# A fused two-layer cross-attention and expert kernel: experts' weights in 48 separately placed parts, and 128 instead of 96 early wide products

## The reference

```
xt = layernorm(x)
router_scores = softmax(xt @ Wr + br)
fs = _grouped_routing_scores(router_scores)   # sort each expert's scores over all tokens, top_k of group sums
up   = einsum('td,edh->teh', xt, Wup) + bup
gate = einsum('td,edh->teh', xt, Wgate) + bgate
h = silu(up) * gate * fs[:, :, None]
x = x + tanh(g_ffn[0]) * (einsum('teh,ehd->td', h, Wdown) + fs @ bdown)
```

## Time and profile before

| | |
|---|---|
| median of 3 runs | 2363.99 us (2362.54 to 2365.33) |
| the profiled execution's own time | 2362.39 us |
| its span, first to last instruction | 2360.6 us |
| busy: PE / DVE / ACT / POOL | 2052.5 (87%) / 1683.4 (71%) / 1228.4 (52%) / 701.8 (30%) us |
| mean granted TensorE clock | 0.922 of full |

### The profile page before, as it was taken

One profiled execution on the slowest core, in us unless ns is written; L12 is line 12 of the kernel. 1 busy time (PEld: TensorE's weight loads), 2 busy tenths in 40 slices (PEclk: granted clock), 3 DMA queues, 4 the chain that ended last, 5 costly groups with the idle time before them and its releaser, 6 DMA issues.

```text
span 2360.6 us, 39296 instructions
## 1 busy us (share of the span) xinstructions
PE 2052.5 (87%) x14938; PEld 1253.5 (53%) x14938; DVE 1683.4 (71%) x2778; ACT 1228.4 (52%) x2950; POOL 701.8 (30%) x568
## 2 busy tenths in 40 slices
PE   5687888887876639999999999999999997899896
PEld 2242555555544424444566666666666655676643
DVE  3558667575787879986566777677777767776688
ACT  1365776867844427555433333333333346677575
POOL 0334866768745627000000000000000003244363
PEclk6788989989987759999999999999999999899997
DMA  4222000000000029454565454454455552000002
GB/s 136 70 72 63 2 1 2 2 1 2 3 1 1 1 69 329 202 220 183 196 190 162 148 161 151 149 160 152 148 163 151 152 164 76 1 2 1 1 1 72
DMA packets 125117, 221.80 MB, mean 94 GB/s; under 512 B 16844, under 2 KB 61761, under 8 KB 124801
## 3 DMA queue, kind: packets, MB, share of 16 engines
q1 hardware_dynamic: 109826, 168.32, 23.5%
q10 hardware_dynamic: 15103, 50.97, 5.4%
HBM read 152.50 MB, written 65.67 MB: 92 GB/s over the span
## 4 chain that ended last, share of the span: by engine, by line
PE 52%; DVE 29%; ACT 12%; issue 4%; DMA 1%; POOL 1%; SPq 0%; ACTq 0%; DVEq 0%; POOLq 0%
PE ps L454 49%; DVE arena L969 14%; DVE arena L978 7%; ACT arena L1916 5%; DVE arena L972 4%; PE ps L462 3%; ACT arena L1668 3%; DVE arena L985 2%; DVE arena L975 1%; ACT arena L1924 1%; ACT arena L1770 1%; ACT arena L1771 1%; POOL arena L2038 0%; DVE arena L988 0%; ACT arena L1672 0%
## 5 line engine op out<-in xcount | busy, mean ns | idle before, releaser
L454 PE MATMUL ps<-arena 128*128 128x512 f16 (+10 forms) x13708 | 1908.8, 299 | 158.4 <-ACT arena L1668 37.2
L454 PEld LDWEIGHTS ps<-arena 128*128 128x128 f16 (+6 forms) x13708 | 1104.7, 102 | 882.0 <-issue 131.2
L969 DVE TENSOR_TENSOR arena<-arena 128x512 f32<-128x512 f32 (+7 forms) x959 | 720.6, 780 | 162.8 <-ACT arena L1874 111.6
L1668 ACT ACTIVATE arena<-ps,arena 128x512 f32<-128x512 f32 (+2 forms) x480 | 319.9, 687 | 191.7 <-PE ps L454 153.4
L1981 POOL TENSOR_TENSOR arena<-arena 128x4 f32<-128x4 f32 (+3 forms) x50 | 85.1, 1703 | 1100.7 <-DVE arena L972 1099.8
L969 DVE TENSOR_TENSOR arena<-ps,arena 128x512 f16<-128x512 f32 (+10 forms) x428 | 227.8, 553 | 247.0 <-ACT arena L1672 62.7
L1874 ACT CAST arena<-arena 128x512 f16<-128x512 f32 x256 | 158.2, 618 | 457.1 <-DVE arena L969 455.1
L2038 POOL TENSOR_TENSOR arena<-arena 128x512 f16<-128x512 f32 (+1 forms) x288 | 346.1, 1221 | 110.8 <-ACT arena L1668 109.3
L462 PE MATMUL ps<-arena 128*128 128x128 f32 (+2 forms) x1230 | 209.6, 303 | 144.8 <-DVE arena L972 61.5
L975 DVE SCALAR_TENSOR_TENSOR arena<-ps,arena 128x512 f32<-128x512 f32 (+4 forms) x302 | 209.2, 695 | 157.3 <-PE ps L454 109.9
L1668 ACT ACTIVATE arena<-ps 128x512 f16<-128x512 f32 (+1 forms) x512 | 273.5, 607 | 73.9 <-PE ps L454 69.5
(11 more groups left out here) (84 smaller groups left out, 496.7 us busy)
## 6 DMA issues: line engine op xcount, KB each, us to landing
arena<-share_scratch SPq DMA_DIRECT2D x512, 128.0 KB, 3.0
wide_scratch<-arena ACTq DMA_DIRECT2D x96, 512.0 KB, 2.6
arena<-wide_scratch SPq DMA_DIRECT2D x96, 512.0 KB, 4.5
mq_scratch<-arena SPq DMA_DIRECT2D x16, 308.0 KB
vw_scratch<-arena SPq DMA_DIRECT2D x32, 154.0 KB
arena<-mq_scratch SPq DMA_DIRECT2D x16, 308.0 KB, 6.1
arena<-vw_scratch SPq DMA_DIRECT2D x8, 576.0 KB, 6.6
arena<-in_x SPq DMA_DIRECT2D x4, 1024.0 KB, 11.5
```

Source lines behind the costliest of these rows:

```text
L454: return e.matmul(o, l, r, start=start, stop=stop, skip_group_check=True)
L969: return e.tensor_tensor(o, a, b, op)
L1668: return e.activation(o, i, f, bias=bias, scale=scale)
```

## The change

- `EARLY` goes from 96 to 128 pairs: groups 0 to 3 are early, groups 4 to 7 widened. In stage 4 there are now 128 widened and 128 reloaded units, strictly in turn.
- The first 44 early products (`EP`, `TAIL = 44`) move into `ORDER`, with due times 295.9 to 322.6, that is from the last gathering on, between the last output projection (PA, PB of the last batch), the routing of group 7, and the last transposes for the sort (`SP`, `SS`), which are now in `ORDER` too.
- Early products go by `EARLIES`: columns 0 to 7 of groups 0 and 1 first, then their other columns, then groups 2 and 3.
- Groups 0 and 1 use the router's turned rows, kept in buffers of their own: two `group_norm` and two `group_turn` are gone. Turn 2 and turn 3 stand at products 36 and 84 of `HOIST`, the first count after 128, and 43 products and turn 4 after the last share.
- The weights are 48 tiles of [128, 1024] fp16. The first four loads (columns 0 to 7) are issued when the last batch's gathering begins and are cast and subtracted in the last batch (due 229.4, 236.4, 243.4, 250.4); eight more when the gathering has ended (due 296.9 to 308.1); the last twelve after the routing.
- The output projection of the last half batch uses PSUM bank 2 in place of 7; `bd` and small constants are prepared after the sort.

```diff
+        o += [(216 + 13 + 7 * n, "W1", n) for n in range(4)] + [(296.5 + 1.6 * n, "W1", 4 + n) for n in range(8)]
+        o += [(295.5 + 0.62 * n, "EP", n) for n in range(TAIL)]
+        o += [(317.2, "SP", 1)] + [(318.4 + 0.7 * q, "SS", q) for q in range(4)]
...
-    SORT_EARLY = 40
+    SORT_EARLY, TAIL = 40, 44
...
+    R = area(q0_, c0_ - 4096)
+    M = area(BASE, c0_ - 4096)
+    MXT = [[M.take([2, 512], F16) for _ in range(2)] for _ in range(2)]
+    RXT = MXT + [(XTh, XTl), [R.take([2, 512], F16) for _ in range(2)]] * 3
...
+    WPART = [PARTS["first"].take([1024], F16) for _ in range(8)] + [PARTS["then"].take([1024], F16) for _ in range(13)]
+    WPART += set_parts + out_parts + low_parts
...
-    EARLY = 96
-    HOIST, at = [("turn", 0), ("turn", 1)], 0
+    EARLY, AHEAD = 128, 4
+    EARLIES = [(g, c) for c0 in (0, 8) for g in range(2) for c in range(c0, 8 if c0 == 0 else 32)]
+    EARLIES += [(g, c) for g in (2, 3) for c in range(32)]
+    HOIST, at = [], TAIL
...
-    for steps_, then in ([(80, [("turn", 2)]), (58, [])] + [(0 if i == 0 else 2, [("count", i)]) for i in range(11)]
+    for steps_, then in ([(36, [("turn", 2)]), (48, [("turn", 3)])] + [(44 if i == 0 else 2, [("count", i)]) for i in range(11)]
                          + [(2, [("rank",)]), (7, [("above",)]), (3, [("tied",)]), (5, [("shares", 0), ("shares", 1)])]
-                         + [(1, [("share", q)] + [("shares", q + 2)] * (q < 2)) for q in range(4)] + [(4, [("turn", 3)])]):
+                         + [(1, [("share", q)] + [("shares", q + 2)] * (q < 2)) for q in range(4)]):
...
-    HOIST += early_until(2 * EARLY)
-    UNITS = weave([(g, c, 0) for g in range(3, 8) for c in range(32)], [(g, c, 1) for g in range(3) for c in range(32)])
+    HOIST += early_until(2 * EARLY) + [("turn", 4)]
+    UNITS = weave([(g, c, 0) for g in range(AHEAD, 8) for c in range(32)], [(g, c, 1) for g in range(AHEAD) for c in range(32)])
...
     def early(n, gate):
-        g, c = divmod(n, 32)
+        g, c = EARLIES[n]
         W.wait_ge("wl", 4 * (c // 8 + 1))
...
-        W.wait_ge("w1", 112)
-        at = 0
+        at = 12
...
-                while at < min(24, 5 + x[1]):
+                while at < min(24, x[1] - 6):
                     weight(at)
...
+        def staging(n):
+            z, st, before = staged(n)
+            if before:
+                W.wait_ge("wl", n - 1 if n < 4 else n - 3)
+            load("g%d" % z, st, W1JOBS[n][0])
+
+        W.wait_ge("ga", 216)
+        load("w1", bup, I["bup"])
+        load("w1", bgt, I["bgate"])
+        for n in range(4):
+            staging(n)
+        W.wait_ge("ga", 288)
+        for n in range(4, 12):
+            staging(n)
         for k in range(2):
             load("w1", bd[64 * k:64 * k + 64, :], I["bdown"])
+        W.wait_ge("rsc", 8)
+        for n in range(12, 24):
+            staging(n)
```

More of the change, by code:

```diff
@@ L140, in emit @@
     XTh, XTl = L.take([2, 512], F16), L.take([2, 512], F16)
+    id16, MN = L.take([128], F16), L.take([4, 8], F16)
     q0_ = L.at
@@ L725, in early, with EP, SS @@
                 empty[4 + n % 2] = [("sil", n + 1)]
+        def EP(i):
+            early(i // 2, i % 2)
+        def SS(q):
+            bk = (2, 3, 0, 1)[q]
+            claim(bk)
+            W.wait_ge("rsc2", 8)
+            for t in range(4):
+                m = tp(bank(bk)[:, 128 * t:128 * t + 128], SCt2[:, 4 * q + t].rearrange("p h e -> p (h e)"), ident)
+            m.then_inc(S["sT"], 1)
+            empty[bk] = [("sS", q + 1)]
+        do = {"C0": C0, "C2": C2, "C3": C3, "C5": C5, "PT": PT, "PU": PU, "PV": PV, "TU": TU, "PJ": PJ, "TR": TR, "MX": MXT_,
+              "QB": QBT, "SC": SCO, "GA": GA, "PA": PA, "PB": PB, "RT": RT, "RC": RC, "SP": SPT, "EP": EP, "SS": SS}
+        for x in ORDER:
+            if x[0] in do:
+                do[x[0]](*x[1:])
         def count(s_):
@@ L821, in narrow @@
                 m = mm3(o, [Hh[q][:, 128 * t:128 * t + 128], Hl[q][:, 128 * t:128 * t + 128]],
-                        [WD[0][:, c, :], WD[1][:, c, :]], False, c == 31 and t % 2 == 1)
+                        [WD[q][c // 4][:, c % 4, :] for q in range(2)], False, c == 31 and t % 2 == 1)
             m.then_inc(S["nar"], 1)
@@ L1301, in vector, with group_norm, group_turn @@
                 do[x[0]](*x[1:])
-        W.wait_ge("rsc", 8)
+        def group_norm(g):
+            W.wait_ge("xT", 2 * (14 + g))
+            normed(mxh, g % 8)
+        def group_turn(g, k, bk):
+            turned_lo(MXT[g % 2][0], MXT[g % 2][1], k, bk, 14 + g)
+        group_norm(2)
+        for n, (lv, k) in enumerate([(lv, k) for lv in range(10) for k in range(lv + 1)]):
+            if n >= SORT_EARLY:
+                SX(0, lv, k)
+        for lv in range(10):
+            if lv == 8:
+                for k in range(2):
+                    group_turn(2, k, 2 + k)
+                group_norm(3)
+            for k in range(lv + 1):
+                SX(1, lv, k)
+        mirror(0, 2048, 1024, B2, B1)
+        src, dst = B1, B2
+        for lv in range(9, -1, -1):
+            spread(0, 2048, 1 << lv, src, dst, None if lv else "routed")
+            src, dst = dst, src
+        assert src is B1
+        for k in range(2):
+            group_turn(3, k, 2 + k)
+        group_norm(4)
         W.wait_ge("w1", 112)
@@ L1842, in early, with EP, SS @@
                     keep(n - 1)
+        def EP(i):
+            if i == 0:
+                W.wait_ge("w1", 80)
+            early(i // 2, i % 2)
+        def SS(q):
+            W.wait_ge("sT", q + 1)
+            e.copy(SC[:, 512 * q:512 * q + 512], bank((2, 3, 0, 1)[q])).then_inc(S["sS"], 1)
+        do = {"C2": C2, "C3": C3, "C5": C5, "PT": PT, "PU": PU, "PV": PV, "TU": TU, "EV": EV, "VH": VH, "NR": NR, "TR": TR, "QB": QBT, "SC": SCO,
+              "PA": PA, "RT": RT, "RC": RC, "SP": SPT, "W1": weight, "EP": EP, "SS": SS}
+        for x in ORDER:
+            if x[0] in do:
+                do[x[0]](*x[1:])
         def share(q):
```

203 lines of the change are left out of this document (74 added, 129 removed).

## The result

| | before | after |
|---|---|---|
| median | 2364.53 us of 4 (2362.54 to 2365.33) | 2323.44 us of 4 (2320.73 to 2328.70) |
| ratio to before | | **0.983**, 95% interval 0.9811 to 0.9850 |
| the profiled execution's own time, its span | 2362.39, 2360.6 us | 2328.70, 2326.9 us |
| busy: PE / DVE / ACT / POOL | 2052.5 / 1683.4 / 1228.4 / 701.8 us | 2052.8 / 1659.3 / 1249.8 / 701.6 us |

A forecast was written before the change was run, and what follows sets the result against it. PE was taken to bound the experts and the stretch beside the sort, but to idle in the hole from 817 to 883. Terms -83.3 + 30.0 + 4 + 2 + 5 + 4 = -38.3 us against 2362.4 gave 2324, range 2307 to 2348.

The forecast's parts named there:

- Removed from the experts: Experts: 32 pairs fewer at 2.603 us of PE each, -83.3 us if PE still bounds that stage.
- the ring: Experts: DVE's combine, ACT's high part, DVE's low part need 5.02 us against PE's 5.22 a pair; loss mostly hidden, +4.
- The hole: PE's mostly idle, half-clock stretch from 817 to 883: filled with 44 products, it ends at 890, including a 3 us wait.
- The last batch, +5: Last batch: four weights' casts on ACT and low parts on POOL, which DVE meets, cost between 0 and 9.1 us, taken +5.
- The early stage: Hole's end to experts: first count at 1058.7 with DVE early by 14 us, experts' start at 1183.7 for 1153.7, +30.0 us.
- +4 for the weights: Early stage: weights 12 to 15 cast in one go and the 16th waiting cost PE 0 to 8 us, taken +4.
- POOL against DVE: Sort: each POOL low part costs DVE 1.73 us; the sort meets 12 instead of 24 and is 20 us shorter.
- All stalls hidden: Rival: last batch absorbs the four weights, casts and turns fit; -53.3 us, 2309; chance 0.12.
- The hole fills badly: Rival: ACT stands at a weight's transfer, group 7 is turned 10 to 15 us later, PE idles; 2339; chance 0.15.
- The ring bounds: Rival: in the experts residuals and transfers stretch the pair from 5.22 to 5.35 us, 17 us more; 2341; chance 0.17.
- The experts keep their old pace: Rival: late shares slow the experts' units; 2385 at 2.85 us a unit, 2424 at 3.0; chance 0.05.
- The change does what it says: Rival denied it: hole's products run only after it as weights or a bank come late; 0 to +15; chance 0.02.

The follow-up runs named there:

- experiments 5 to 7: Changed kernel with redundant short DVE operations in each widened unit: one copy, an addition and a copy, four additions; 2326.20, 2323.97 and 2390.84 us.
- experiment 3: Changed kernel with POOL's low parts of the first four weights set to zero by memset instead of subtracted; 2324.40 us (one run).
- experiments 8 and 9: Changed kernel with the first 11, and the first 30, late compare steps of the sort done twice; 2323.17 and 2350.22 us (one run each).
- experiment 1: Changed kernel with the 44 products moved out of the hole to behind the routing, 128 pairs still early; 2356.41 us, ratio to before 0.9966.
- experiment 2: Changed kernel with 96 pairs early instead of 128, 44 of their products still in the hole; 2333.37 us, ratio to before 0.9878.
- kernel 6: Changed kernel with a redundant DVE addition of 128 columns and a copy of 64 in each widened unit; 2323.97 us (one run).
- kernel 7: Changed kernel with four redundant DVE additions of 128 columns in each widened unit; 2390.84 us (one run).

## Why the prediction was right

Forecast 2324 us with a range of 2307 to 2348; measured 2323.4. The sum was -38.3 us, the medians differ by -41.1; the number is nearer than the sum, since before's executions here have a median 2 us above the one that I summed against. Half a microsecond is luck: the stages that the change leaves alone scatter by 8 and 5 us. The mechanism is what the runs bear out: by rows, from the last batch to the end of the experts, the change is worth 41.3 us in the profile laid beside before. By its own steps:

- **Removed from the experts, -83.3, with +4 for the ring.** Together -79.3; measured 692.7 - 771.2 = -78.5. The total is right and the +4 is on the wrong cause. The ring, residuals and normed rows took nothing: the pair stayed at 5.22 with its 0.20 of slack, and experiments 5 to 7 show that it would have bound from there on. What was lost, 5.57 us and some clock behind it, was a share behind the eight loads. I had covered shares "at the median, not at 5.5" and had not looked for what makes them late: the burst at unit 10. It stood in before too, where a share had 8.3 us of room and not 7.1, and where PE lost 2.3 us to DVE in all.
- **The hole.** Its end was put 73 us behind the last gathering; the 44th product, counted by matmuls, ends at 895.3 and the gathering at 822.3: 73.0. The stop ahead of group 7 was put at 3 us and is 1.99, with a granted clock of 0.58 from 863 to 866 that the sum had not. Group 7's turning was to come 9.6 us later beside the last batch's +5, 14.6 in all; it came 863.10 - 849.32 - 2.8 = 11.0 later.
- **The last batch, +5.** Measured +2.6 (its last gathering at 822.3 - 2.8 for 816.9), and 0.35 without the low parts (experiment 3). In the profile that is half of the term, but the twelve traces of experiment 3 have a median of 3.7, so it was mis-sized by less. That more of the four blocks of 1.73 fell into DVE's idle time than I took is argued, not shown.
- **The early stage.** From the hole's end to the first count 172.1 us, the sum had 168.6 and +4 for the weights; the waits for ACT are 1.85 + 1.26 = 3.1. DVE was to be early by 14 us and was by 17.80; experiments 8 and 9 show the slack by using it up. From first count to last share 67.9 us, as the 68 before. Turn 4: 1.80 for +2.
- **The experts' start** came 40.0 us later, or 37.2 without the set-up's 2.8; the terms for it made 41.0. That is where the -38.3 was 3 us too careful.
- **The table loads.** ACT in the hole goes to exp and back:

```profile
870.18 0.69 ACT L1692 ACTIVATE arena<-ps,arena 128x512 f32<-128x512 f32 x1 [0.67 <-PE ps L478]
...
870.89 1.28 ACT L1692 ACT_TABLE_LOAD   x1
872.27 0.42 ACT L1692 ACTIVATE arena<-arena 128x256 f32<-128x256 f32 x1
```

The operation before ends at 870.87 and exp starts at 872.27: 1.40 us for the switch. The prediction summed with the row's 1.28, and that held. By the rule of the Trainium skill ("ScalarE: Activation LUTs", "What ACT_TABLE_LOAD costs"), a drain would make it an estimated 2.66 and the hole 76 us; the trace does not show the drain, and the hole took 73.0.
- **POOL against DVE.** DVE and POOL, grouped by form, from 875 to 1010:

```profile
L997 DVE TENSOR_TENSOR arena<-arena 128x512 f32<-128x512 f32 x140 | 111.3, 837 | 2.4
```

```profile
L2079 POOL TENSOR_TENSOR arena<-arena 128x1024 f16<-128x1024 f32 x12 | 28.3, 2378 | 23.0 <-ACT arena L1835 23.0
```

Against 689 ns alone, 140 operations lost 140 x 0.148 = 20.7 us, and over 12 of POOL's that is 1.73 each, the number that before gave for 24: the sort's 20 us were rightly summed. By the full lock that the Trainium skill describes ("SBUF — State Buffer", "SBUF: two separate sides") it would be an estimated 28.3 us, POOL's whole time in the row, and DVE's other operations in the stretch may hold the rest; the rows of 1024 columns don't tell. Between 829 and 846, where DVE has six operations of 512 columns and idles for the most part, four of the same subtractions took POOL 2.00 us each and not 2.38, so POOL's own rows are longer beside DVE as well.

**The rivals.** All stalls hidden: no, 1.99, 3.1, 1.80 and 5.57 us are in the rows. The hole fills badly: no, PE is busy 0.96 of it. The ring bounds: no, by a margin of 0.20 us a pair. The experts keep their old pace: no, 199 GB/s were carried, with a share's landing at a median of 3.7 us for 3.0 and a reload's at 4.8; what it named, a late share that holds a combine, happened once. The change does what it says: experiment 1 takes the hole away and loses 33 us.

## What to carry to other kernels

A stage in which one engine is busy to 0.99 is not made faster inside; look for the idle time of that engine elsewhere and ask what may be computed there, and count the clock in: transposes in the hole halved, and the waits of 4 to 22 us in experiments 2 and 9 and in after are followed by some 5 us at 0.50 to 0.61 of the clock, so a stall costs more than its length. Then follow each moved product to the resource that frees it (weights in small parts, a bank, a store), because the waits that come new are of that kind, and small. And a queue that is covered at the median is asked next what else is issued in it at once: here one burst of loads cost 5.57 us of waiting, where 4 had been put down for a ring with 4% of slack that took nothing.

## What the runs showed of the hardware

- Short DVE operations overlap one another: additions of 128 columns have rows of 284 ns (mean in kernel 6), and four of them put off the next operation by 0.18 us each (kernel 7). A row's length is no measure of what one more short operation costs.
- The transfers of 128 KB shares landed in 3.0 us (median) at 158 GB/s, and in 3.7 at 199 GB/s. The mix of transfers differs between the two, so the 0.7 us are not shown to be the load's alone; in the experts PE had no wait over 1 us behind their first one, but for the one at the eight larger loads.
- A switch of ACT's tables took 1.40 us from the end of one operation to the start of the next, 1.28 of it the load.
- The granted clock is low right behind a wait of PE: 0.50 from 1089 to 1095 after 22.14 us (experiment 9), 0.50 from 1045 to 1050 after 9.88 (experiment 2), 0.61 from 1235 to 1240 after 5.57 (after), and 1.00 in the stretch that follows the last of these.
- A POOL subtraction of 1024 columns took 2.00 us beside a mostly idle DVE and 2.38 beside DVE's additions of 512 columns, which lost 1.73 us to each.
